# Closing the row maxima of an attention kernel in half units, 13 steps ahead of their use

## The reference, cut to what matters

```
hid = group_norm(x, 32 groups) * norm_w + norm_b              # per image
q, k, v = split(qkv_w @ hid + qkv_b)                          # 8 heads of 16 channels
weight = softmax(q.T @ k * 16**-0.5, axis=-1)                 # 1024 x 1024 per head
x = x + proj_w @ (v @ weight.T) + proj_b
# second layer, per image:
x = x + conv_w @ gelu(rmsnorm(x, norm1_w)) + conv_b
x = x + ffn_w2 @ gelu(ffn_w1 @ rmsnorm(x, norm2_w) + ffn_b1) + ffn_b2
```

## Time and profile before

| what | value |
|---|---|
| median of three executions | 1805.92 us (1805.7 to 1807.43) |
| the profiled execution: its own time | 1808.65 us |
| its span, first to last instruction | 1806.8 us |
| mean granted TensorE clock | 0.969 of full speed |
| busy: TensorE matmul, VectorE, ScalarE, GpSimd | 1734.7, 1463.3, 1399.5, 290.0 us |

### The profile page before, as it was taken

How to read it: one execution, slowest core, us unless ns; L and a number is a source line. 1 busy time by engine, 2 the same in 40 slices (tenths; PEclk the granted TensorE clock), 3 DMA queues, 4 the chain that set the end, 5 groups by cost and what they waited for, 6 DMA issues and landing times.

```text
span 1806.8 us, 32324 instructions
## 1 busy us (share of the span) xinstructions
PE 1734.7 (96%) x12178; PEld 701.8 (39%) x12178; DVE 1463.3 (81%) x2318; ACT 1399.5 (77%) x2608; POOL 290.0 (16%) x283
## 2 busy tenths in 40 slices
PE   4999999999999999999999999999999998699998
PEld 2433333333333333333333333333333332355555
DVE  4899989898989898989898989898989961455552
ACT  1078888888888888888888888888888888466664
POOL 3010111111111111111111111111111001322220
PEclk7589999999999999999999999999999999699999
DMA  6080606060605060606050606050606001233332
GB/s 116 10 211 9 90 8 91 8 90 8 91 8 90 8 90 8 90 8 90 8 90 8 90 8 90 8 90 8 90 8 91 9 22 36 73 106 106 106 106 71
DMA packets 53835, 106.17 MB, mean 59 GB/s; under 512 B 26032, under 2 KB 28976, under 8 KB 53680
## 3 DMA queue, kind: packets, MB, share of 16 engines
q1 hardware_dynamic: 51376, 95.72, 30.7%
q10 hardware_dynamic: 2304, 8.39, 1.1%
HBM read 34.54 MB, written 9.06 MB: 24 GB/s over the span
## 4 chain that ended last, share of the span: by engine, by line
PE 85%; DVE 6%; issue 3%; ACT 3%; DMA 1%; SPq 1%; POOL 1%; DVEq 0%; ACTq 0%; POOLq 0%
PE psum L591 27%; PE psum L619 26%; PE psum L603 10%; PE psum L685 6%; DVE maxes L870 5%; PE psum L573 4%; PE psum L657 2%; PE psum L659 2%; PE psum L658 2%; PE psum L560 2%; PE psum L514 2%; ACT probs L802 1%; PE psum L702 1%; DVE stats L889 1%; ACT k_high L788 1%
## 5 line engine op out<-in xcount | busy, mean ns | idle before, releaser
L870 DVE TENSOR_REDUCE maxes<-psum 128x1 f32<-128x512 f32 x2048 | 1280.0, 684 | 142.9 <-PE psum L591 136.7
L802 ACT ACTIVATE probs<-psum 128x512 f32<-128x512 f32 x2048 | 1101.2, 603 | 211.7 <-PE psum L603 186.9
L591 PE MATMUL psum<-k_stack,q_stack 62*128 62x512 f32 x2048 | 793.2, 467 | 16.9 <-DVE maxes L870 9.1
L603 PE MATMUL psum<-q_stack,k_stack 64*128 64x512 f32 x2048 | 777.7, 458 | 1.4 <-ACT probs L802 1.1
L619 PE MATMUL psum<-probs,values 128*32 128x256 f32 (+1 forms) x6656 | 614.2, 441 | 0.6 <-ACT probs L802 0.4
L591 PEld LDWEIGHTS psum<-k_stack,q_stack 62*128 62x128 f32 x2048 | 326.4, 189 | 563.9 <-DVE maxes L870 513.4
L603 PEld LDWEIGHTS psum<-q_stack,k_stack 64*128 64x128 f32 x2048 | 312.5, 185 | 32.3 <-ACT probs L802 20.9
L619 PEld LDWEIGHTS psum<-probs,values 128*32 128x32 f32 x6656 | 131.1, 108 | 277.2 <-issue 225.1
L685 PE MATMUL psum<-probs,inv_den 128*128 128x512 f32 x256 | 116.5, 598 | 0.0
L811 ACT ACTIVATE probs<-psum,params_sb 128x512 f32<-128x512 f32 x128 | 82.7, 687 | 21.8 <-PE psum L659 15.4
L454 POOL TENSOR_TENSOR q_low<-q_full,q_high 128x1024 fp32r<-128x1024 f32 x16 | 38.0, 2376 | 317.1 <-ACT q_high L788 317.1
(11 more groups left out here) (84 smaller groups left out, 995.3 us busy)
## 6 DMA issues: line engine op xcount, KB each, us to landing
q_stack<-q_high SPq DMA_DIRECT2D x128, 128.0 KB, 3.8
k_stack<-k_high SPq DMA_DIRECT2D x128, 128.0 KB, 5.0
x_sb<-in_x SPq DMA_DIRECT2D x16, 512.0 KB, 9.9
q_stack<-q_low SPq DMA_DIRECT2D x64, 128.0 KB, 6.1
k_stack<-k_low SPq DMA_DIRECT2D x64, 128.0 KB, 6.7
attn<-raw SPq DMA_DIRECT2D x128, 64.0 KB, 2.5
inv_den<-inv_den_rows SPq DMA_DIRECT2D x128, 64.0 KB, 2.2
values<-inv_rms_rows SPq DMA_DIRECT2D x16, 512.0 KB, 4.8
```

What stands on the lines that cost most here:

```text
L591: nc.tensor.matmul(psum[:, BANKS + tile % BANKS, :], q_stack[rows, place, p, 128 * chunk:128 * chunk + 128], k_stack[rows, place, p, HALF ...
L603: nc.tensor.matmul(psum[:, tile % BANKS, :], k_stack[rows, place, p, 128 * chunk:128 * chunk + 128], q_stack[rows, place, p, HALF * t:HALF ...
L802: nc.scalar.activation(probs[:, tile % 8, :], psum[:, tile % BANKS, :], ACT.Exp, scale=SCALE).then_inc(probs_ready, 1)
L870: nc.vector.tensor_reduce(maxes[:, (2 * p + j) * NK + chunk, key_half:key_half + 1], psum[:, BANKS + max_tile(u, s, k) % BANKS, :], axis=A ...
```

## The change

The maxima now run LEAD = 13 steps ahead of the scores (22 before), and they are closed by half a unit (one t) rather than by a unit. VectorE closes a half at step 3 or 11 (`close_half`) behind the second tile; GpSimd makes the high part by a copy and the low part by a subtraction (`maximum_parts`); VectorE turns both by four transpositions of 32 x 32 blocks after the tiles of step 4 or 12 (`turn_half`); SyncE moves them by two DMAs. The transposition on TensorE, both copies on ScalarE and the identity matrix are gone, and step 11 is no longer broken.

ScalarE writes q and k once, in full; GpSimd rounds them by a copy ahead of its subtraction (`split`). `q_stack` is split by query half, so the stack of a unit takes 18 DMAs: 12 of 64 KB for q and 6 of 128 KB for k. The fourth q and k step is 13, not 14. The statistics of image b + 3 are at steps 3, 6 and 7 of half 1; the reciprocal is at step 6. SyncE's order is: heads, the rows of t = 1, the inverse sums, the second stack, the rows of t = 0 of the next unit, and in half 1 the first stack and then one image of x. Three images are loaded at the start instead of four. `refine(-4)` comes after step 6 of the last unit (ahead of its step 0 before) and `refine(-3)` after step 12 (after step 9 before).

```diff
-LEAD = 6
+LEAD = 13
-STACK_DMAS, ROW_DMAS, HEAD_DMAS, WEIGHT_DMAS = 12, 8, 8, 7
+STACK_DMAS, ROW_DMAS, HEAD_DMAS, WEIGHT_DMAS = 18, 2, 8, 6
-QK_STEPS = (3, 6, 10, 14)
-SIDE_STEPS = ((3, 4, 6, 9, 11, 13, 15), (3, 6, 10, 11, 14))
+EARLY_X = 3
+QK_STEPS = (3, 6, 10, 13)
+SIDE_STEPS = ((3, 4, 6, 9, 13, 15), QK_STEPS)
...
-            if s + LEAD < STEPS:
-                return u + 1, (2 * parity + half + 1) % RING, s + LEAD
-            return u + 2, (2 * parity + half + 2) % RING, s + LEAD - STEPS
+            return divmod(u * STEPS + s + LEAD, STEPS)
...
@@ SyncE: stack, maximum_rows, slot @@
+                            for t in range(NT):
+                                sp.dma_start(q_stack[at:at + CH, (2 * c + half) % RING, t, :, :].bitcast(fp32),
+                                             part[lines, HALF * t:HALF * t + HALF].bitcast(fp32)).then_inc(stack_in, 16)
+            def maximum_rows(v, t):
+                sp.wait_ge(rows_ready, NT * v + t + 1)
+                at_least(sp, rows_in, (NT * v + t) * (16 * ROW_DMAS))
+                for j in range(2):
+                    at = ROWS * j + MAX_ROW
+                    row = q_stack[at:at + 2, v % RING, t, :, :].bitcast(fp32).rearrange("n p f -> n (p f)")
+                    sp.dma_start(row.rearrange("n (k f) -> n k f", f=128),
+                                 rows[16 * j:16 * j + 16, :].bitcast(fp32)).then_inc(rows_in, 16)
...
+                if has_unit(u) and part in (None, 1):
+                    maximum_rows(u, 1)
                 if half == 0 and has_image(b - 1) and part in (None, 1):
...
+                if half == 0 and has_image(b + 1):
+                    at_least(sp, scores_ready, u * TILES)
+                    stack(b + 1, 1)
                 if has_unit(u + 1):
+                    maximum_rows(u + 1, 0)
                 if half == 1 and has_image(b + 2):
+                    at_least(sp, scores_ready, u * TILES)
+                    stack(b + 2, 0)
+                if half == 1 and EARLY_X <= b + 5 < IMAGES:
+                    at_least(sp, x_rest_in, 16 * (b + 5 - EARLY_X))
+                    load_x(b + 5, x_rest_in)
...
@@ GpSimd @@
+            def maximum_parts(v, t):
+                n = NT * v + t
+                pool.wait_ge(neg_max_ready, n + 1)
+                at_least(pool, rows_ready, n)
+                nc.gpsimd.tensor_copy(parts[:, :, 0, :], neg_max[:, :, :]).then_inc(high_ready, 1)
+                pool.wait_ge(high_ready, n + 1)
+                nc.gpsimd.tensor_tensor(out=parts[:, :, 1, :], in0=neg_max[:, :, :], in1=parts[:, :, 0, :].bitcast(fp32),
+                                        op=ALU.subtract).then_inc(parts_ready, 1)
+            def split(full, high, low, c, n):
+                pool.wait_ge(qk_full, 4 * c + 2 * n + 2)
+                at_least(pool, stack_in, c * (2 * 16 * STACK_DMAS))
+                nc.gpsimd.tensor_copy(high[:, :], full[:, :]).then_inc(qk_high, 1)
+                pool.wait_ge(qk_high, 2 * c + n + 1)
                 nc.gpsimd.tensor_tensor(out=low[:, :], in0=full[:, :], in1=high[:, :].bitcast(fp32),
                                         op=ALU.subtract).then_inc(split_done, 1)
...
@@ TensorE, scores @@
-                if s == 0 and k == 0:
-                    pe.wait_ge(rows_in, u * (16 * ROW_DMAS) + 16 * ROW_DMAS)
+                if chunk == 0 and k == 0:
+                    pe.wait_ge(rows_in, (NT * u + t + 1) * (16 * ROW_DMAS))
...
@@ ScalarE, side_jobs @@
-                    for out in (full, high):
-                        last = nc.scalar.activation(out[:, half_image], qk_bank(b, n), ACT.Identity,
-                                                    bias=params[:, bias:bias + 1])
-                    last.then_inc(qk_full, 1)
+                    nc.scalar.activation(full[:, HALF * (n % 2):HALF * (n % 2) + HALF], qk_bank(b, n), ACT.Identity,
+                                         bias=params[:, bias:bias + 1]).then_inc(qk_full, 1)
...
@@ VectorE @@
+            def close_half(n):
+                dve.wait_ge(max_taken, (n + 1) * (TILES // NT))
+                at_least(dve, parts_ready, n)
+                nc.vector.tensor_reduce(neg_max[:, :, :], maxes[:, n % NT, :, :, :], axis=AX.X, op=ALU.max,
+                                        negate=True).then_inc(neg_max_ready, 1)
+            def turn_half(n):
+                dve.wait_ge(parts_ready, n + 1)
+                at_least(dve, rows_in, n * (16 * ROW_DMAS))
+                for q in range(4):
+                    last = nc.vector.transpose(
+                        rows[:, 32 * q:32 * q + 32].bitcast(fp32),
+                        parts[32 * q:32 * q + 32, :, :, :].rearrange("q j n c -> q (j n c)").bitcast(fp32))
+                last.then_inc(rows_ready, 1)
+                        if closes and k == 1:
+                            close_half(half_unit - 1)
...
+                if half == 1 and has_image(b + 3):
+                    if s in (3, 6):
+                        statistics(b + 3, s // 6)
+                    if s == 7:
+                        statistics_of_both(b + 3)
-                if s == 5 and has_image(b - 1):
+                if half == 0 and s == 6 and has_image(b - 1):
...
@@ the last unit @@
+            for part in range(2):
+                slot(IMAGES - 1, 1, 1, part)
             refine(-4)
-            for part in range(3):
-                slot(IMAGES - 1, 1, 1, part)
+            slot(IMAGES - 1, 1, 1, 2)
             refine(-3)
```

More of the change, by code:

```diff
@@ L149, in build @@
         out_bias = sb("out_bias", [128, 1])
[L150 to L154, removed]
+        group_mean = sb("group_mean", [128, C])
+        maxes = sb("maxes", [128, NT, 2, 8, 2])
+        neg_max = sb("neg_max", [128, 2, 8])
+        parts = sb("parts", [128, 2, 2, 8], fp32r)
+        rows = sb("rows", [32, 128], fp32r)
         stats = sb("stats", [128, 2, 6])
@@ L199, in qk_bank @@
             return psum[:, n, :] if fills(b) else misc
-        weights_in, x_in = sem("weights_in"), [sem(f"x_in{n}") for n in range(4)]
+        weights_in, x_in = sem("weights_in"), [sem(f"x_in{n}") for n in range(EARLY_X)]
         x_rest_in = sem("x_rest_in")
@@ L346, in slot @@
+                    at_least(sp, heads_in, (u - 1) * (16 * HEAD_DMAS))
                     heads(1 - half)
-                if half == 0 and has_image(b + 1):
-                    at_least(sp, scores_ready, scored)
-                    at_least(sp, stack_in, stacked)
-                    stack(q_rounded, rounded, split, 1 - parity, 1)
-                if is_first(b) and half == 0:
-                    for n in range(4, IMAGES):
-                        load_x(n, x_rest_in)
+                if has_unit(u) and part in (None, 1):
+                    maximum_rows(u, 1)
@@ L458, in slot @@
                 u = b * 2 + half
+                if has_unit(u) and part in (None, 1):
+                    maximum_parts(u, 1)
                 if half == 0:
@@ L578, in wait_for_bank, with maximum_scores @@
                 at_least(pe, freed, tile - BANKS + 1)
-            def maximum_scores(u, parity, half, s, k):
-                unit, place, step = max_item(u, parity, half, s)
+            def maximum_scores(u, s, k):
+                unit, step = max_item(u, s)
+                place = unit % RING
                 if not has_unit(unit):
@@ L590, in maximum_scores @@
                 wait_for_bank(tile, max_taken)
-                nc.tensor.matmul(psum[:, BANKS + tile % BANKS, :], q_stack[rows, place, p, 128 * chunk:128 * chunk + 128],
-                                 k_stack[rows, place, p, HALF * key_half:HALF * key_half + HALF],
+                nc.tensor.matmul(psum[:, BANKS + tile % BANKS, :],
+                                 q_stack[used, place, chunk // 4, p, 128 * (chunk % 4):128 * (chunk % 4) + 128],
+                                 k_stack[used, place, p, HALF * key_half:HALF * key_half + HALF],
                                  start=True, stop=True).then_inc(max_ready, 1)
@@ new lines, in side_jobs @@
+            def side_jobs(b, parity, half, s):
+                if half == 1 and has_image(b + 3):
[3 more added lines that the diff above has]
+                        statistics_of_both(b + 3)
+                if half == 0 and fills(b) and s == 0:
+                    statistics(0, 0)
+                    statistics(0, 1)
+                    statistics_of_both(0)
+                    nc.vector.memset(k_stack[:, :, :, :].bitcast(fp32), 1.0).then_inc(stacks_set, 1)
+                if half == 0 and s == 6 and has_image(b - 1):
```

206 lines of the change are left out of this document (74 added, 132 removed).

## The result

| | before | after |
|---|---|---|
| median, same chip | 1806.68 us (1805.70 to 1808.40, 4 executions) | 1763.62 us (1763.44 to 1764.15, 4 executions) |
| ratio after to before, 95% interval | | 0.9761 (0.9744 to 0.9778) |
| span of the profiled execution | 1806.8 us | 1761.8 us |
| mean granted TensorE clock | 0.969 | 0.975 |
| first maximum tile, first scores | 35.93, 96.19 us | 36.03, 75.52 us |

Forecast were 1758 and 1745 to 1787, faster. Run again in another job it gave 1763.48 us, ratio 0.9757 (0.9743 to 0.9772). An image begins with its first score tile and has 32 steps.

What follows compares the result with a forecast made beforehand. TensorE's program and its waits, mostly for VectorE, were taken as the bound. Start -18, images 1 to 13 -31, image 0 -1.2, image 14 -0.6 and end +3 gave -47.8: 1758 us on the median's side, range 1745 to 1787.

Steps and rivals of the forecast that it cites:

- start: Up to the first scores: nine steps fewer -21.7, later first stack +1.6, VectorE's statistics, closing and turn +2.1; sum -18.0 us.
- image 0: First image: its slower matmuls already hide its statistics, so it gains only part, -1.2 us.
- images 1 to 13: Images with all of the gain: 13 x -2.4, or -31 us.
- image 14: Last of the fifteen images, with neither statistics nor q and k: -0.6 us.
- from image 15 to the end: Nine steps become slower, +1.4 us; heads queue 1.6 us behind the later `refine(-3)`; sum +3 us.
- Removals of an image: Per image: statistics -1.04, ScalarE's second rounding -0.6, step 11 of half 1 -0.8, transposition in half 0 -0.2 us.
- What VectorE gets: Four closings and four turns an image, 0.4 us a turn, mostly absorbed: +0.3 us an image (0 to 2.0).
- Rival (a): VectorE's turns come through: 0.5 us for each of about 60 turns, +26 us, 1784 us; chance 15%.
- (b): SyncE's rows wait mildly behind the stack, 1.5 to 3 us late in 14 images: about 1789 us; chance 6%.
- (c): 2 KB rows of q cost as much as 4 KB, delaying SyncE's rows: 1814 to 1884 us, slower; chance 7%.
- Rival (d): The shorter lead moves starvation from the start into the main part, steps 0 and 8: around 1805 us; chance 2%.
- Its own signs: First scores near 78, image about 88.0, transposition near 0.1 us; wrong if image over 89 or first scores after 84.

Runs made afterwards that it cites:

- changed_again: The changed kernel run again in another job, with no edit, against the kernel before: 1763.48 us, ratio 0.9757.
- act_rounds: The changed kernel with ScalarE rounding q and k again by a second activation and GpSimd only subtracting: 1774.82 us, ratio 0.9822 to the kernel before.
- stats_early: The changed kernel with the statistics of image b + 2 back at steps 0 and 1 of half 0: 1774.64 us, ratio 0.9827 to the kernel before.
- turn_quarter: The changed kernel with one small transposition a turn instead of four: 1750.83 us, ratio 0.9694 to the kernel before.
- turn_twice: The changed kernel with every 32x32 transposition done twice, once into a spare tile: 1817.64 us, ratio 1.0068 to the kernel before.
- old_stats_moved: The kernel before with its statistics alone moved to steps 3, 6 and 7 of half 1: 1791.96 us, ratio 0.9917 to the kernel before.
- stack_first: The changed kernel with SyncE's second stack ahead of the rows of t = 1 and the inverse sums: 1895.54 us, ratio 1.0488 to the kernel before.
- lead_21: The changed kernel with the maxima 21 steps ahead instead of 13: 1781.57 us, ratio 0.9857 to the kernel before.

## Why the prediction was right, and where it was off

The sign, the size and the mechanism held: 45.0 us between the two spans where 47.8 were forecast. The total is closer than its parts, as misses cancel: the fifteen images gave 8.4 us less than forecast, start and end 5.6 more. By its steps:

| step | forecast | measured |
|---|---|---|
| start | -18.0 | -20.7 |
| image 0 | -1.2 | +0.3 (-0.4 in changed_again) |
| images 1 to 13 | -31 (-2.4 each; its terms add up to -2.34) | -25.4 (-1.95 each) |
| image 14 | -0.6 | +0.75 |
| from image 15 to the end | +3 | +0.1 |

- *Start.* Nine steps fewer were worth what was said: the first nine of the kernel before take 21.3. The later stack (+1.6) hides behind an earlier begin: from the first transfer of the stack to the first maximum tile it is 15.27 us against 14.17, with GpSimd's copy at 1.04, but that transfer goes out at 20.76 against 21.76, so the tile comes at 36.03 against 35.93. Why the work ahead of it began earlier stays open; it also varies between executions (the first copy of the group mean on ScalarE comes at 10.65, in act_rounds at 12.45). VectorE's +2.1 showed in part: the 13 steps take 39.49 us, and 38.21 in stats_early, so the two statistics and their joining are paid with 1.3; the turn, just ahead of a broken step, costs nothing (39.48 in turn_quarter and in turn_twice).
- *Removals of an image.* Statistics -1.04 forecast, -1.07 in the steps and -1.15 in old_stats_moved; ScalarE's rounding -0.6, measured -0.59; step 11 of half 1 -0.8, measured -0.79; step 11 of half 0 -0.2, measured -0.23. These four terms were read off step lengths, and all came within 0.15.
- *What VectorE gets: the term that was mis-sized.* I took 0.1 for each small transposition and 0.6 us for the lag that is absorbed. The transposition takes 0.198, near the other end of my bounds (0.22), and a turn 0.76. I had given as a reason that the four need not drain between them; in the trace each begins 13 ns after the one before it has ended, while two reductions of 512 columns in a row overlap by 82 ns. Step 5 of half 1 pays what is beyond about 0.2. The term was +0.3 an image and measured about +0.8 (0.57 + 0.16 + 0.07), and that is the miss of the images. The 0.6 was read off steps 1 to 3 of half 0, whose last is broken. The same turn costs 0.07 behind the broken step 4 of half 0, nothing behind the plain step 12 with the broken 13 next, and 0.48 by itself behind step 4 of half 1, where it and step 5 are both plain.
- *Images 0 and 14.* Step 13 has no job of TensorE there (in half 0 of image 0, in half 1 of image 14), and then it pays for its turn: it takes 3.48 or 3.49 with four transpositions, 3.05 with two and 2.75 with one. I had given both images a part of the gain only, without this cost.
- *End.* The last steps cost nearly the +1.4 that was forecast (image 15's steps +1.2). The heads did queue behind `refine(-3)`, by 1.0 us where 1.6 was forecast. First the kernel before, where they go out as soon as ScalarE has copied the last result, then the changed one, where they wait for one more transfer of `refine(-3)`:

```profile
1530.88 0.59 ACT L747 COPY raw<-psum 128x512 f32<-128x512 f32 x1 [1.19 <-PE psum L619]
1531.49 0.53 SPq L321 DMA_DIRECT2D attn<-raw  x1
...
1487.01 0.58 ACT L735 COPY raw<-psum 128x512 f32<-128x512 f32 x1 [1.19 <-PE psum L607]
1488.17 0.33 SPq L389 DMA_DIRECT2D values<-inv_rms_rows  x1
1488.60 0.53 SPq L327 DMA_DIRECT2D attn<-raw  x1
```

  What gave most of the +3 back is the stretch from the last matmul of the projection to the end, 242.25 us against 243.96. Of that the change need not be the cause: in old_stats_moved, which does not touch the end, the same stretch takes 241.64. So the total of this row is in part luck.
- *Rival (a)*, turns that come through, happened in a small part: its transposition of 0.22 came nearly true (0.198), but GpSimd's parts were not late (VectorE waited 0.6 us for them in the whole run), and a turn came through once an image at 0.5 to 0.6, not 60 times at 0.5. turn_twice shows that it would have been the whole story at twice the work: slower than before.
- *Rivals (b) and (c)* did not happen. In the order of the queue the rows were issued at 823.99 to 825.30 and used from 829.50, with no wait. The margin was thinner than the 4 us of the prediction: from the first issue of these rows to their use there are 4.6 to 6.7 us in images 1 to 14 (7.6 forecast), and in stack_first, where TensorE waited for such a pair, the issue was 2.9 to 4.1 us ahead of its next tile. By these rows the margin is about 2 us, an estimate. A row of 2 KB did not cost what one of 4 KB does: from a stack's first issue to its last landing it is 15.5 us (median, 18 transfers) against 14.1 to 14.6 (12 transfers), where (c) wanted 22, and the high parts of q landed in 2.2 us each at 64 KB where they took 3.8 at 128 KB. The Trainium skill, "DMA: Bandwidth & Descriptors", section "Why small descriptors are slow (HBM only)", says that transfers within SBUF don't suffer that penalty; the trace agrees. stack_first shows that the place was rightly chosen: rows behind a stack cost 132 us.
- *Rival (d)*: lead_21 has the same images, so the shorter lead moved no starvation into them.
- *Its own signs.* The bounds at which it called itself wrong (an image over 89 us, first scores after 84) were kept. Missed were the transposition near 0.1 us and the image of about 88.0.

The Trainium skill, "VectorE: DVE Perf Modes", section "Rules for kernel authors", calls VectorE's transposition the fastest for 32 x 32. For one block the trace agrees, 0.198 us against 0.27 for TensorE's one matmul. But a turn takes four of them, 0.76 us for half a unit, where that one matmul served a whole unit, so the transposition itself became dearer. What the change gained at step 11 was TensorE's job with its wait, 0.23 us in half 0 and 0.79 in half 1.

What stays open: why 0.2 us are absorbed, whether by the banks' lead or by the order of the tiles in a step (I did not vary the number of banks), and why the stretch from the last matmul of the projection to the end differs by 2 us between executions.

## What to carry to other kernels

Where two engines are level, read the cost of an edit from the lengths of the steps around it: these terms came true to a tenth of a microsecond, while the one term with an operation that no row showed missed by a factor of two. Put side work of the engine that is level inside the steps in which the other one has a side job too; a turn then cost nothing here, and 0.5 us between plain steps. Ask also what a shorter lead brings close together: rounding on ScalarE was free of waits with 22 steps of lead and cost 6 us at the start with 13. Before moving a transfer in a shared queue, count the issues behind which it comes to stand.

## What the runs showed of the hardware that I had not expected

- A transposition of 32 x 32 in fp32 on VectorE took 0.198 us, about as long as the reduction of 128 x 32 to 128 x 16 (0.182) that works on four times the partitions. Four in a row did not overlap (13 ns from the end of one to the start of the next), while reductions of 512 columns overlapped by 82 ns.
- With three banks of lead about 0.2 us of VectorE's lag was absorbed, not 0.6, where the lag arose behind a plain step and the next one was plain too.
- After a stall of 6 us the granted clock was 0.51 for 4.3 us with TensorE busy all the while (0.79 us for the matmul that takes 0.50), so each such stall was paid with about 2.2 us on top (median of 13 images; 2.7 by the mean).
- SyncE issued a transfer within SBUF every 0.62 to 0.68 us whether it moved 64 or 128 KB; the 18 of a stack took 11.8 us.
